# Head 0 and the first pair prepared in the first FFN, two batches normalised in attention's first steps, one table load per root

## The reference

```
x = x + 0.5 * ffn(layernorm(x))     # 8 experts of 176 hidden units, top 2 of 8 weigh them
x = x + attention(layernorm(x))     # 16 heads of complex dimension 64
x = x + 0.5 * ffn(layernorm(x))
```

## Time and profile before

| | us |
|---|---|
| median of 3 runs | 1802.85 (1801.56 to 1804.66) |
| profiled execution, its own time | 1803.02 |
| span of the profiled execution | 1801.2 |
| PE busy | 1673.7 (93%) |
| DVE busy | 1465.6 (81%) |
| ACT busy | 1462.5 (81%) |
| POOL busy | 986.3 (55%) |
| ACT table loads, 23 in number, of 1.283 each | 29.5 |

### The profile page before, as it was taken

The page is one execution under the profiler, slowest core; times in us unless marked ns, Lnnn a source line. Parts: engine busy times, 40 slices in busy tenths (PEclk is TensorE's granted clock), DMA queues, the critical chain, the costliest instruction groups (busy, mean ns, idle before and its releaser), DMA issues. The chain is left out here.

```text
span 1801.2 us, 30230 instructions
## 1 busy us (share of the span) xinstructions
PE 1673.7 (93%) x9664; PEld 1338.4 (74%) x9664; DVE 1465.6 (81%) x3202; ACT 1462.5 (81%) x2815; POOL 986.3 (55%) x841
## 2 busy tenths in 40 slices
PE   5998976999999999999999999999999999789998
PEld 3786754877787777778777778777877787667876
DVE  6777866788889888988988888898888889767675
ACT  5777765989989898998989899898989998665765
POOL 3554544556565555656565655566556556235565
PEclk9999988999999999999999999999999999889999
DMA  6000013132213222222222222232222222100000
GB/s 166 1 1 1 2 69 76 47 74 57 65 48 74 64 58 71 50 74 48 74 53 69 62 59 73 49 73 49 74 62 59 63 59 48 24 1 13 12 7 18
DMA packets 42974, 92.26 MB, mean 51 GB/s; under 512 B 7360, under 2 KB 19264, under 8 KB 42816
## 3 DMA queue, kind: packets, MB, share of 16 engines
q1 hardware_dynamic: 42816, 90.33, 20.1%
HBM read 17.95 MB, written 5.24 MB: 13 GB/s over the span
## 5 line engine op out<-in xcount | busy, mean ns | idle before, releaser
L1247 POOL TENSOR_TENSOR rot<-by_cos,crossed 128x1024 f32<-128x1024 f32 x128 | 304.9, 2382 | 499.0 <-PE pS L1062 269.2
L1255 POOL TENSOR_TENSOR ek<-decay,knorm 128x128 f32<-128x128 f32 (+3 forms) x512 | 431.2, 876 | 30.1 <-ACT knorm L1172 29.9
L593 POOL TENSOR_TENSOR hid_lo_d<-hid_d,hid_hi_d 128x512 fp32r<-128x512 f32 x176 | 230.8, 1311 | 242.2 <-ACT hid_hi_d L511 235.6
L1164 ACT ACTIVATE z<-z,nmax 128x128 f32<-128x128 f32 (+3 forms) x512 | 281.3, 552 | 86.8 <-DVE nmax L1302 86.8
L1302 DVE CUSTOM_DVE_ANT_0 z<-u,lam,hp 128x128 f32<-128x128 f32 (+3 forms) x512 | 255.8, 556 | 110.0 <-ACT u L1192 109.1
L1062 PE MATMUL pS<-rot 128*128 128x128 f32 (+3 forms) x1024 | 298.0, 434 | 0.4 <-ACT probT L1187 0.4
L1180 ACT ACTIVATE u<-u,qnorm 128x128 f32<-128x128 f32 (+3 forms) x512 | 246.1, 551 | 53.4 <-DVE u L1314 49.0
L1062 PEld LDWEIGHTS pS<-rot 128*128 128x128 f32 x1024 | 165.3, 192 | 95.9 <-issue 62.0
L1311 DVE SCALAR_TENSOR_TENSOR pS<-pS,ek 128x1280 f32<-128x1280 f32 x128 | 191.8, 1498 | 52.8 <-PE pS L1062 52.8
L1097 PEld LDWEIGHTS pS<-ident,z 128*128 128x128 f32 x1280 | 141.7, 142 | 83.8 <-ACT z L1164 53.9
L1097 PE MATMUL pS<-ident,z 128*128 128x128 f32 x1280 | 166.0, 277 | 39.7 <-DVE u L1314 32.7
(11 more groups left out here) (239 smaller groups left out, 3558.7 us busy)
## 6 DMA issues: line engine op xcount, KB each, us to landing
crossed<-by_sin SPq DMA_DIRECT2D x256, 256.0 KB, 3.6
cos<-trig_d SPq DMA_DIRECT2D x64, 64.0 KB, 2.2
sin<-trig_d SPq DMA_DIRECT2D x64, 64.0 KB, 2.1
raw_d<-in_w SPq DMA_DIRECT2D x3, 704.0 KB, 9.0
x_sb<-in_x SPq DMA_DIRECT2D x4, 512.0 KB, 8.6
wqk_raw<-in_wqk SPq DMA_DIRECT2D x16, 128.0 KB, 3.6
out_x<-x_sb SPq DMA_DIRECT2D x8, 256.0 KB, 2.3
trig_d<-cos_t_d SPq DMA_DIRECT2D x1, 1024.0 KB, 4.4
```

What stands on the lines that cost most here:

```text
L593: g.tensor_tensor(hid_lo[:, par], hid[:, par], hid_hi[:, par].bitcast(F32), ALU.subtract).then_inc(lo_done, 1)
L1164: last = a.activation(z[:, span(I)], z[:, span(I)], ACT.Exp, bias=nmax[:, I:I + 1], scale=-1.0, accum_out=rsum[:, r % 4, I:I + 1])
L1247: g.tensor_tensor(rot[:], by_cos[:], crossed[:], ALU.add).then_inc(S["rot_done"], 1)
L1255: last = g.tensor_tensor(ek[:, span(I)], decay[par][:, span(I)], knorm[:, 0:(I + 1) * P], ALU.mult)
```

## The change

1. `root` loads the set that holds both Ln and Exp itself, once, ahead of its wait for the variance. Before, only the start of a dense phase did so.
2. The first head's weights, angles and parameters are loaded and prepared in the first FFN: SP's transfers behind the stores of the angle tables, the split on ACT at slot 83 and DVE at slot 85, decay argument at slot 78. Their buffers and those of the first pair lie in `s.early`, which is one region with the raw weights and the angle tables of the FFN.
3. The projection of pair 0 stands on PE ahead of the last down product; `by_sin`, `by_cos`, the crossing and the squares of pair 0 follow in the FFN's block. Attention starts at step -1 and no longer loads a table at its start.
4. Moments of batch 7, root, refinement, normalising, transposing and splitting of batches 6 and 7 (`late_...`) move from the FFN's end into attention's steps -1, 0 and 1. The projections of pairs 6 and 7 wait for them, and the first `weigh` too, since it writes the bank `p7` that they pass through.

```
@@ dense_phase, SP, behind the stores of the tables
                 sp.wait_ge(trig_out, 48)
+                sp.wait_ge(wp_lo, 4)
+                sp.dma_start(s.wqk_raw, s.wqk[0]).then_inc(s.S["w_in"], 16)
+                for q, table in enumerate((1, 2, 2, 1)):
+                    rows = slice(q * DH // 2, (q + 1) * DH // 2)
+                    sp.dma_start(s.cos0[rows, :], s.trig_d[0, 0]).then_inc(s.S["trig_in0"], 16)
+                    sp.dma_start(s.sin0[rows, :], s.trig_d[table, 0]).then_inc(s.S["trig_in0"], 16)
+                sp.wait_ge(s.S["bs_done"], 1)
+                sp.dma_start(s.crossed[0:DH, :], s.by_sin[DH:P, :]).then_inc(s.S["crossed_in"], 16)
+                sp.dma_start(s.crossed[DH:P, :], s.by_sin[0:DH, :]).then_inc(s.S["crossed_in"], 16)
+                sp.wait_ge(s.S["crossed_in"], 32)
@@ PE, behind the last slot
+            if first:
+                pe.wait_ge(gated_done, SLOTS)
+                pe.wait_ge(xlo_done, B + 1)
+                pe.wait_ge(s.S["w_hi"], 1)
+                pe.wait_ge(s.S["w_lo"], 1)
+                for j in range(2):
+                    last = mm3(pe, s.pQK[:, j * N:(j + 1) * N], tuple(h[:, j * P:(j + 1) * P] for h in s.wqk0),
+                               (s.xT[0][:, 0:N], s.xT[1][:, 0:N]), True, True)
+                last.then_inc(s.S["qk_done"], 1)
             down(SLOTS - 1)
             turn_y(B - 1)
-            if first:
-                pe.wait_ge(hid_done, SLOTS)
-                turn_x(B + 6, w_bank[0])
-                turn_x(B + 7, w_bank[1])
@@ ACT
             def root(n, b0, b1):
+                nc.scalar.preload_act_table_set("natural_log_exp_and_others")
                 a.wait_ge(var_done, n + 1)
...
+                if first and e == 83:
+                    a.wait_ge(s.S["w_in"], 16)
+                    a.activation(s.wqk0[0], s.wqk_raw, ACT.Copy).then_inc(s.S["w_hi"], 1)
...
+            if first:
+                nc.scalar.preload_act_table_set("natural_log_exp_and_others")
+                a.wait_ge(s.S["arg_done"], 1)
+                a.activation(s.decay0, s.decay0, ACT.Exp).then_inc(s.S["decay_done"], 1)
             copy_out(B - 1)
             if first:
-                root(5, 6, B)
-                a.wait_ge(rstd_done, 6)
-                normalise(B + 6, 0, TILES)
-                normalise(B + 7, 0, TILES)
-                high(B + 6, w_bank[0])
-                high(B + 7, w_bank[1])
+                a.wait_ge(s.S["cos_done"], 1)
+                a.activation(s.squares, s.pQK[:], ACT.Square).then_inc(s.S["sq_done"], 1)
@@ DVE
+                if e == 77:
+                    v.tensor_copy(s.hp0, s.params[:, 0, :]).then_inc(s.S["hp_done"], 1)
+                if e == 78:
+                    v.wait_ge(s.S["hp_done"], 1)
+                    ts(s.decay0, s.dist[:], s.hp0[:, NEG_MU:NEG_MU + 1], MIN_EXP, ALU.mult,
+                       ALU.max).then_inc(s.S["arg_done"], 1)
+                if e == 85:
+                    v.wait_ge(s.S["w_hi"], 1)
+                    tt(s.wqk0[1], s.wqk_raw, s.wqk0[0].bitcast(F32), ALU.subtract).then_inc(s.S["w_lo"], 1)
+            if first:
+                v.wait_ge(s.S["trig_in0"], 128)
+                v.wait_ge(s.S["qk_done"], 1)
+                tt(two(s.by_sin), two(s.pQK[:]), both(s.sin0), ALU.mult).then_inc(s.S["bs_done"], 1)
+                tt(two(s.by_cos), two(s.pQK[:]), both(s.cos0), ALU.mult).then_inc(s.S["cos_done"], 1)
             add_out(B - 1)
-            if first:
-                moments_out(B - 1)
-                aggregate_out(B - 1)
-                variance(6, B)
-                refine(5, 6, B, y_bank[0])
-                low(B + 6, w_bank[0])
-                low(B + 7, w_bank[1])
@@ attention_phase
-        FIRST, STEPS, TAIL = -2, 2 * B, 5
+        FIRST, STEPS, TAIL = -1, 2 * B, 5
@@ SP
-            load(0, 0)
@@ PE, in a_step, behind project; weigh(0) waits for late_lo 2, project of pairs 6 and 7 for late_lo 1 and 2
+                if i == 0 and r in (0, 1):
+                    turn_x(r)
@@ ACT: where the new functions stand in a_step
+            def late_root():
+                a.wait_ge(S["late_var"], 1)
+                a.activation(s.late_root, s.late_var, ACT.Ln).then_inc(S["late_ln"], 1)
+                a.wait_ge(S["late_ln"], 1)
+                a.activation(s.late_root, s.late_root, ACT.Exp, scale=-0.5).then_inc(S["late_root"], 1)
+            def late_normalise(j):       # four activations, as in normalise
+            def late_high(j):            # as high, from p7
                 if live(i, r + 1):
                     key_norms(i, r + 1)
+                if i == 0 and r == -1:
+                    build(LN, 0, 0)
+                if i == 0 and r == 0:
+                    late_normalise(0)
+                    late_normalise(1)
                 if live(i, r):
                     clamp(i, r)
...
                 if live(i, r):
                     logs(i, r)
+                if i == 0 and r in (0, 1):
+                    late_high(r)
...
+                if i == 0 and r == -1:
+                    late_root()
-            nc.scalar.preload_act_table_set("natural_log_exp_and_others")
-            for part in (EXP, LN):
-                build(part, 0, 0)
@@ POOL: build(0, 0) from ahead of the steps to the end of step -1
@@ DVE
             def a_step(i, r):
+                if i == 0 and r == 0:
+                    late_refine()
                 if live(i, r - 1):
                     peaks(i, r - 1)
...
                     build_back(i, building(MASK, i, r))
+                if i == 0 and r == -1:
+                    late_moments()
+                if i == 0 and r == 0:
+                    build_back(0, 0)
+                if i == 0 and r in (0, 1):
+                    late_low(r)
-            build_front(0, 0)
-            build_weights(0, 0)
-            build_back(0, 0)
```

More of the change, by code:

```diff
@@ L145, in dense_phase @@
             half_pi = sb("half_pi", [P, 1])
-            angle, cos_t, sin_t, nsin_t = (sb(n, [P, 4, N]) for n in ("angle", "cos_t", "sin_t", "nsin_t"))
+            angle, cos_t, sin_t, nsin_t = (
+                s.early[:, 3 * HC * P + k * 4 * N:3 * HC * P + (k + 1) * 4 * N].rearrange("p (g t) -> p g t", g=4)
+                for k in range(4))
             head_sem, wr_in, ident_in, w13_in, w2_in, angle_in, cst_in, wvo_in = (sem(n) for n in (
@@ L955, in attention_phase @@
         sem = lambda name: ctx.enter_context(nc.semaphore(name))
-        decay = [sb(f"decay{k}", [P, SW]) for k in range(2)]
-        decay2 = sb("decay2", [P, N])
-        lam = [sb(f"lam{k}", [P, N]) for k in range(2)]
-        cos = [sb(f"cos{k}", [P, N]) for k in range(2)]
-        sin = [sb(f"sin{k}", [P, N]) for k in range(2)]
-        hp = [sb(f"hp{k}", [P, NPAR]) for k in range(2)]
-        wqk_raw = sb("wqk_raw", [P, 2 * P])
-        wqk = [[sb(f"wqk_{half}{k}", [P, 2 * P], F32R) for half in ("hi", "lo")] for k in range(2)]
-        by_cos = sb("by_cos", [P, 2 * N])
-        by_sin = sb("by_sin", [P, 2 * N])
-        crossed = sb("crossed", [P, 2 * N])
-        squares = sb("squares", [P, 2 * N])
-        rot = sb("rot", [P, 2 * N])
-        knorm = sb("knorm", [P, N])
+        decay = (s.decay0, sb("decay1", [P, SW]))
+        lam = (s.lam0, sb("lam1", [P, N]))
+        cos = (s.cos0, sb("cos1", [P, N]))
+        sin = (s.sin0, sb("sin1", [P, N]))
+        hp = (s.hp0, sb("hp1", [P, NPAR]))
+        wqk = (s.wqk0, [sb(f"wqk1_{half}", [P, 2 * P], F32R) for half in ("hi", "lo")])
+        decay2, wqk_raw, by_cos, by_sin, crossed = s.decay2, s.wqk_raw, s.by_cos, s.by_sin, s.crossed
+        squares, rot, knorm, u, z = s.squares, s.rot, s.knorm, s.u, s.z
         qnorm = sb("qnorm", [P, 2, TILES])
         ek = sb("ek", [P, SW])
-        u = sb("u", [P, SW])
-        z = sb("z", [P, SW])
         probT = [sb(f"probT{k}", [P, SW]) for k in range(2)]
@@ L981, in attention_phase @@
         stats = sb("stats_at", [P, TILES, 6])
[L982 to L986 removed]
+        S = s.S
         trig_in = (S["trig_in0"], S["trig_in1"])
@@ L1109, in values, with turn_x @@
                 last.then_inc(S["v_done"], 1)
+            def turn_x(j):
+                pe.wait_ge(S["late_xn"], j + 1)
+                wait(pe, S["late_lo"], j)
+                for q in range(TILES):
+                    last = pe.transpose(s.p7[:, q * P:(q + 1) * P], late_xn[j][:, q * P:(q + 1) * P], s.ident[:])
+                last.then_inc(S["late_xt"], 1)
             def weigh(i, r):
                 n = i * 16 + r
+                if n == 0:
+                    pe.wait_ge(S["late_lo"], 2)
                 wait(pe, S["trc_done"], n + 1)
@@ L1207, in values_out @@
                 last.then_inc(S["val_done"], 1)
+            def late_root():
[4 more added lines that the diff above has]
+            def late_normalise(j):
+                a.wait_ge(S["late_rstd"], 1)
+                for q in range(TILES):
+                    k = j * TILES + q
```

(25 more changed lines are left out.)

54 lines of the change are left out of this document (43 added, 11 removed).

## The result

The changed kernel takes 1786.88 us (median of 4 runs, 1785.39 to 1787.41) against 1802.2 for the kernel before (4 runs); the ratio is 0.9911, 95% interval 0.9894 to 0.9928, so 15.3 us faster by the medians and 16 by the ratio, between 13 and 19. The forecast was 1784.5, range 1780 to 1791. The profiled execution is the fastest of the four, 1785.39 us with a span of 1783.6, which is 17.6 less than before; the other three have spans of 1785.1 to 1785.6 and a mean granted clock of 0.984 to 0.985 instead of 0.987. The two profiled executions, 1803.02 before and 1785.39 after, are 17.6 us apart; the medians are 15.3 apart because the one before was 0.8 us slower than its median and the one after 1.5 us faster.

The account below looks back on a forecast made before the run. Bounds seen: PE's table-load waits at the FFN's roots and the serial hand-over to attention, whose long stretch only shifts. 17.75 - 4.7 + 5.15 + 0.7 - 0.5 = 18.4 us, giving 1784.5 us, range 1780 to 1791.

Parts of the forecast that it names:

- one load per root: Roots 1 to 4 of the first FFN: Ln and Exp share one table load, about 5.15 us won (4.2 to 5.2).
- clock behind root 4: First FFN, 223 to 227 us: with a shorter PE wait the clock may stay up, 0.7 us won (0 to 1.6).
- the last slots: Head-weight split and decay argument moved into the FFN's last slots: 0.5 us lost (0 to 1.5), transfers at nothing.
- the new end: FFN's end: projection goes in early, the crossing sets the block's end, attention's norms start 17.75 us sooner.
- given back in attention: Attention's first steps: late work of batches 6 and 7 delays them, 4.7 us lost (3.5 to 6.5).
- The drain: Rival at table switches: about 1380 ns more per load, gain 23.9 us, 1779.1 us; chance 0.02.
- the rival in which the roots give nothing: DVE takes the limit behind the roots: gain 13.05, 1789.9 us; within "less won", chance 0.13.
- The second stage: Attention: ACT's high and DVE's low half of batch 6 come ahead of the peaks of pair 0, 1.1 us net.
- The third: Attention, one step on: the same two halves for batch 7 come ahead of the peaks of pair 1, 0.5 us more.
- three signs of being wrong: Loads inside attention, ACT waiting at slot 83, or peaks of pair 1 less than 12 us sooner, roots aside.
- The slower rival: Attention's 128 steps each load two tables because none is carried over: 195 us more, near 1980 us; chance 0.04.
- The weaker one: Late chain in attention wholly in series: 10.8 instead of 4.7 us lost, 1790.9 us; within "less won", chance 0.13.

Follow-up runs that it names:

- the run with the loads alone: Kernel before with one table load per root and nothing else of the change: 1795.42 us against 1803.04, ratio 0.9956.
- The run without the end wait: Changed kernel without the wait for the crossing at the end of the FFN's block; POOL's addition in attention waits for it instead: 1781.78 us.
- the two other repairs: Low half in slot 87 and late work early; with no wait at the block's end, all three on the changed kernel: 1776.70 us, ratio 0.9858.
- no late work: Changed kernel with moments, root, refinement, normalising, turning and splitting of batches 6 and 7 taken out, output not the reference's: 1780.98 us.

## Why the prediction was right, and where it was off

By its own steps, in profiled executions:

| term | forecast | measured |
|---|---|---|
| one load per root | +5.15 | +5.1 |
| clock behind root 4 | +0.7 | 0 |
| the last slots | -0.5 | -1.1 |
| the new end | +17.75 | +18.0 |
| given back in attention | -4.7 | -4.8 |
| sum | 18.4 | 17.2 |

**The loads.** Right in place and size; the second FFN had shown the after-state. The drain that the Trainium skill has for a switch (ScalarE: Activation LUTs, "What ACT_TABLE_LOAD costs"), as a rival worth 5.5 us more, is refuted by the run with the loads alone; so is the rival in which the roots give nothing.

**The clock behind root 4.** The step "I take 0.7" is mis-sized: the clock stayed up as hoped, but nothing came of it. The old kernel lost 0.8 us to slow matmuls behind root 4 (3.66 us from the first one to the end of the down product's last, 2.86 in the changed kernel), in front of a wait for ACT's expanded weights. With the clock up PE only waits longer there. Before and after:

```profile
226.79 0.79 PE L299 MATMUL pS<-ident,wexp_d 128*128 128x128 f32 x4 [0.19 <-ACT wexp_d L447]
```

```profile
221.69 0.65 PE L311 MATMUL pS<-ident,wexp_d 128*128 128x128 f32 x4 [0.98 <-ACT wexp_d L465]
```

The shift is 5.10 us here, after 5.09 at root 4. A wait stood behind the stretch, and I had not looked which. The step that bound the fall to the length of the wait was weak too: root 1's wait of 2.61 us had drawn no fall in the same profile, and the prediction names only roots 2 and 3 as the waits without one.

**The last slots.** "I charge 0.5 us" is mis-sized, for the low half, which has two operands in SBUF, ran against POOL (1.20 us instead of the 0.4 it takes alone in attention) and pushed the chain hidden product, split, down product by 0.84 us. I had looked for such meetings at attention's peaks alone. The other 0.25 us stays with slot 87 (255.13 - 250.25 = 4.88 us ahead there, 5.13 with the loads alone). The transfers are nine, not the ten of the prediction, and cost nothing as it says: the last lands at 234.55, 8 us ahead of the split. The clock is a further cost that I had nowhere: behind PE's wait of 1.92 us, with twelve matmuls of 512 columns still to come, the clock fell in three of six profiles, for 0.9 to 1.6 us each. That may go towards the 1.5 us between the profiled run and the other runs of the changed kernel, whose clock is lower. Where in those runs it fell no trace shows, and in other profiles it fell at 28 to 34, 40 to 46 and 160 to 167 us of the FFN and in attention's last steps as well. That the profiles gained 17.6 us and the medians 15.3 is a spread of this kind on both sides, argued and not shown for those very runs; when the changed kernel was run again, its median lay 17.9 us under that of the kernel before.

**The new end.** Right: crossing 4.5 us, block's end 0.3 us, everything else hidden (SP issues the crossing at 254.86, and the norms start 4.79 us later). The run without the end wait confirms that the wait sets the start.

**Attention.** The sum, 4.7, was right, and so was the first stage: distances 2.95 us late, forecast 3.25. The second stage was near: the peaks of pair 0 are 3.9 us late, from +15.54 to +19.45, forecast 4.55. The third was not. The peaks of pair 1 are 6.2 us late, from +26.45 to +32.65, forecast 5.05: in between, the peaks of pair 0 met POOL's addition, 2.1 us that the prediction had kept for its bound of 6.5 and not put into the 4.7. By pair 5 some 1.4 us had come back, and how wasn't followed. So the agreement of 4.8 with 4.7 is in part luck. Taking the late work out leaves 0.28 us, and its mere reordering brings back 3.7.

**The signs.** One of the prediction's three signs of being wrong was met. No load stands inside attention, and ACT doesn't wait at slot 83 (its split starts at 242.91, behind an activation that ends at 243.00). But the peaks of pair 1 start at 292.30 instead of 308.07, 15.8 us sooner, or 10.7 with the 5.1 of the roots taken off, and not the 12 that the prediction asks for. The total came out inside the range because of what came back behind them.

**The slower rival,** a table not carried over from phase to phase: no load stands inside attention, so the table of the phase before was still there. **The weaker one,** late work in series, is excluded by 4.8 us.

## What to carry to other kernels

Work that is moved into a fill phase costs little if it goes where each engine stands idle and much if it merely goes behind what was there: the same instructions cost 4.8 us behind by_cos and about 1 us when most of them stood before by_sin, and about half of that difference is a meeting of two other operations which the delay brought about. Before an operation is put into the last slots of a phase, look at what it shares with the neighbour engine and how many products wait behind it, and look for the wait that follows a stretch before counting a speed-up of it as won. A wait that only closes a block is worth a run without it: here, with the two other repairs, it made a kernel of 1776.7 us, 1.4% under the one before. And where executions differ by a microsecond or two, compare them at the end of the stretch that was changed: a chance fall of the clock a thousand microseconds later is in the total too.

## What the runs showed of the hardware

The same PE wait can cost the clock in one execution and not in the next. The granted clock fell (to a mean of 0.57 to 0.67 over the 4 to 5 us behind the wait) after the wait of 2.59 us at root 4 in both profiles that have it, behind that of 2.61 us at root 1 in one of two, behind that of 2.0 us in attention's last steps in eight of thirteen, and behind that of 1.92 us in the FFN's last slots in three of six. With waits of 1.3 us it did not fall at root 4 in any of eleven profiles, but at root 1 it did in one of eleven (no late work, 0.66 in 40 to 45 us). Such a fall cost 1.06 us between the last two pairs of attention and 0.9 to 1.6 us in the last slots, and at root 4 nothing, since PE waited behind it anyway. The mean clock of a run is therefore no measure of what it lost.

A DVE operation with both operands in SBUF that starts just behind the start of a POOL addition (2.34 to 2.42 us alone) waits for the whole of it. The thirteen profiles have 19 such meetings in attention's first steps, with peak operations of 2.56 to 2.57 us (256 wide, otherwise 0.48) or 2.83 (512 wide, otherwise 0.75). POOL's addition had begun 0.13 to 0.63 us earlier, while the peak operation before was still running, and in all 19 it ended 2.27 to 2.29 us after the start of the delayed one, however early it had begun. So the price is the same each time, 2.1 us, and where it falls depends on which peak operation is the next.
